# A GpSimd memset behind every gather of a graph kernel's conv passes

## What is computed

```python
eh  = relu(edge_attr @ en1_w.T + en1_b)              # once: [edges, 128]
w_e = (eh @ en2_w.T + en2_b).reshape(-1, 32, 32)     # a 32x32 matrix for every edge
out = h = relu(x @ lin0_w.T + lin0_b)
for _ in range(6):                                   # six conv steps
    msg = einsum('ei,eio->eo', out[src], w_e)        # out[src]: the gather
    agg = segment_sum(msg, dst, num_segments=6250) + conv_bias
    h = out = gru_cell(relu(agg), h)
```

## Time and profile before

| what | value |
|---|---|
| median of the runs | 24,022.46 us |
| profiled execution, first to last instruction (span) | 30,532.6 us |
| GpSimd busy in it | 14,020.9 us (46%), 16,639 instructions |
| of these the gathers, L785 | 9,408, 8,876.9 us |
| TensorE busy | 18,622.1 us (61%) |
| VectorE busy | 11,720.7 us (38%) |
| ScalarE busy | 7,911.3 us (26%) |
| HBM traffic | 110 GB/s over the span |

### The profile page before, as it was taken

One profiled execution on the slowest core, in us unless ns is written; L12 is line 12 of the kernel. 1 busy time (PEld: TensorE's weight loads), 2 busy tenths in 40 slices (PEclk: granted clock), 3 DMA queues, 4 the chain that ended last, 5 costly groups with the idle time before them and its releaser, 6 DMA issues. The chain is left out here.

```text
span 30532.6 us, 420576 instructions
## 1 busy us (share of the span) xinstructions
PE 18622.1 (61%) x121575; PEld 13266.8 (43%) x121575; DVE 11720.7 (38%) x29589; ACT 7911.3 (26%) x20853; POOL 14020.9 (46%) x16639
## 2 busy tenths in 40 slices
PE   3333555555655676667666766676666766676654
PEld 3333322222244454455444554455445544554444
DVE  5444566666710333233323333233323332333220
ACT  0000344445510222222222322232222222232210
POOL 4886355555610444534453445344443445344520
PEclk5555788888977777777777877787777777787777
DMA  3222233322278222112211221122112221122147
GB/s 97 48 49 69 85 122 118 113 99 93 68 293 344 66 64 59 52 58 65 58 54 53 68 63 55 48 69 63 56 53 60 63 59 54 57 65 60 55 142 308
DMA packets 1398480, 2692.30 MB, mean 88 GB/s; under 512 B 938471, under 2 KB 1104704, under 8 KB 1189106
## 3 DMA queue, kind: packets, MB, share of 16 engines
q10 hardware_dynamic: 335568, 1445.71, 13.4%
q1 hardware_dynamic: 709952, 1053.68, 10.0%
q0 software_dynamic: 352256, 186.21, 4.3%
HBM read 2105.10 MB, written 1242.55 MB: 110 GB/s over the span
## 5 line engine op out<-in xcount | busy, mean ns | idle before, releaser
L785 POOL DMA_INDIRECT sb_xg<-node_rows,sb_src_c x9408 | 8876.9, 944 | 11917.8 <-SPq L803 6579.1
L921 PE MATMUL banks<-sb_work,sb_eh_sb 128*128 128x256 f32 x29184 | 8833.9, 453 | 1693.7 <-issue 1358.2
L921 PEld LDWEIGHTS banks<-sb_work,sb_eh_sb 128*128 128x128 f32 x29184 | 6472.3, 229 | 3674.0 <-issue 2259.6
L874 DVE TENSOR_TENSOR sb_work<-sb_xs,banks_p 128x2048 f32<-128x2048 f32 x1824 | 4171.1, 2288 | 9843.7 <-remote 5895.0
L978 ACT ACTIVATE sb_work<-banks 128x512 f32<-128x512 f32 x7296 | 4124.9, 599 | 11185.0 <-remote 7003.8
L1200 PE MATMUL banks<-sb_hot_code,sb_xs 128*128 128x392 bf16 x7296 | 1874.5, 371 | 2173.7 <-DVE sb_work L1163 1435.1
L1163 DVE SCALAR_TENSOR_TENSOR sb_work<-sb_work,sb_eh_sb,banks 128x784 f32 x2432 | 2502.3, 1029 | 572.4 <-PE banks L1202 484.1
L864 DVE COPY sb_xs<-sb_xg 128x32 f32 x14592 | 1762.7, 191 | 2459.9 <-issue 2268.6
L907 PE MATMUL banks_p<-sb_work,sb_en 128*32 128x256 f32 x29184 | 2084.7, 391 | 778.6 <-issue 766.1
L367 POOL DMA_INDIRECT slots<-sb_rows,sb_slot_u x1600 | 2108.6, 1318 | 786.7 <-issue 762.6
L1079 POOL TENSOR_SCALAR sb_xs<-sb_codes,sb_code 128x128 bf16<-128x128 f16 x2432 | 1516.6, 624 | 2067.3 <-PE banks L1202 2067.1
(11 more groups left out here) (281 smaller groups left out, 13084.1 us busy)
## 6 DMA issues: line engine op xcount, KB each, us to landing
sb_eh_sb<-eh ACTq DMA_DIRECT2D x912, 1024.0 KB
weights_between<-sb_work ACTq DMA_DIRECT2D x305, 1568.0 KB
edges_between<-sb_work ACTq DMA_DIRECT2D x305, 1568.0 KB
sb_work<-weights_between SPq DMA_DIRECT2D x147, 3136.0 KB, 12.5
sb_work<-edges_between SPq DMA_DIRECT2D x98, 3136.0 KB, 12.4
eh<-sb_eh_sb ACTq DMA_DIRECT2D x304, 512.0 KB, 2.6
sb_xg<-node_rows,sb_src_c POOLq DMA_INDIRECT x9408
sb_win_row<-window_rows SPq DMA_DIRECT2D x100, 488.3 KB
```

What stands on the lines that cost most here:

```text
L785: nc.gpsimd.indirect_dma_start(m.xg_ring[:, row % RING * D:(row % RING + 1) * D], None, m.node_dram, bass.IndirectOffsetOnAxis(ap=m.src_c[ ...
L874: V.tensor_tensor(m.spread[q], m.xs[h].rearrange("s (t i) -> s t i", i=D)[:, tiles, :].unsqueeze(3) .broadcast_to([P, TS, D, WN]), m.mask_ ...
L921: o = mm(m.ps_pair[u % 4][:, v, :, :], m.eh[h % 2][:, t * K:(t + 1) * K], m.spread[t // TS][:, t % TS, :, :], start=True, stop=True)
```

## The change

Behind each gather GpSimd now writes zeros to one of two scratch tiles of 128x240 f32, in turn, and counts it on a new semaphore `paused`. From the third gather on, it first waits until the memset before last is done. At the end of a pass's gathers it waits for the last memset. Nobody reads the scratch tiles. Nothing else is touched: the gathers, their order, their semaphores and all other engines' programs stay as they are. The scratch tiles take 1,920 bytes of each partition.

```diff
-def gather_rows(nc, m, pool, got, landed, room, held):
+def gather_rows(nc, m, pool, got, landed, room, paused, held):
...
             nc.gpsimd.indirect_dma_start(
                 m.xg_ring[:, row % RING * D:(row % RING + 1) * D], None, m.node_dram,
                 bass.IndirectOffsetOnAxis(ap=m.src_c[:, row:row + 1], axis=0)).then_inc(got[b % L], 16)
+            if row >= 2:
+                pool.wait_ge(paused, row - 1)
+                hold(pool, held)
+            nc.gpsimd.memset(m.pause[row % 2], 0.0).then_inc(paused, 1)
+    pool.wait_ge(paused, JT)
...
-            gather_rows(nc, m, pool, got, landed, room, held_pool)
+            gather_rows(nc, m, pool, got, landed, room, paused, held_pool)
...
         m.own_now = sb("own_now", [P, D], halves=2)
+        m.pause = sb("pause", [P, 240], halves=2)
```

More of the change, by code:

```diff
@@ L810, in conv_pass @@
                "copied", "masked", "twinned", "made", "summed", "g_done", "g_sb", "s_sb", "grouped", "pj_sb", "folded",
-               "out_sb", "held_dve", "held_pool") as (block, *sems):
+               "out_sb", "paused", "held_dve", "held_pool") as (block, *sems):
         got, eh_in, stored = sems[0:4], sems[4:6], sems[6:10]
         (landed, room, copied, masked, twinned, made, summed, g_done, g_sb, s_sb, grouped, pj_sb, folded, out_sb,
-         held_dve, held_pool) = sems[10:26]
+         paused, held_dve, held_pool) = sems[10:27]
         def skewed(eng, *steps, tail=None, behind=0):
```

## The result

The changed kernel takes 25,500.14 us in the median (25,498.74 to 25,516.16) against 24,026.48 us for the kernel before: 1,474 us more. The ratio on record is 1.0617, 95% interval 1.0602 to 1.0632. The forecast was slower, 26,600 us in a range of 24,700 to 27,400: right in its direction and within its range, but the cost of the memsets was put at 2,579 us, 1.75 times what it is.

The account below looks back on a forecast made before the run. GpSimd's gather pace was taken to bound two thirds of every conv loop. Serial memsets raise a loop from 1,998 to 2,428 us, 2,579 us in all on the 24,022.46 us median: 26,600 us, range 24,700 to 27,400.

Parts of the forecast that it names:

- The timed runs have no stalls, and the gathers' pace bounds most of a loop: Conv loops: timed runs lack the profile's burst stalls; gathers bound two thirds of every loop, other engines the first third.
- The calculated loop: One conv loop without stalls: larger of gathers x 1.249 and batches x 11.85 in three stretches, 1,998 us; fill and tail 11.
- The wait and the hold cost nothing: GpSimd's sequencer, per gather: cost zero, as it needs 0.46 of each 1.249 us and the hold takes 17 ns.
- never dry: GpSimd's cores: with the lead cut to two gathers they still have 1.25 us of work; the sequencer needs 0.46.
- The memset's own time, 0.298 us: Per gather on GpSimd: 0.10 us for one column plus 239 x 0.83 ns; between 0.10 and 0.374 us.
- The memset goes serially with the gathers: GpSimd's cores make both, so the gather period becomes 1.249 + 0.298 = 1.547 us; chance 0.70.
- the rival of the gap: The memset fits into the 0.30 us between gathers and costs nothing: 24,022 to about 24,100 us; chance 0.10.
- the forecast's own sum: One loop's three stretches at 1.547 us a gather: 767 + 784 + 876 = 2,428 against 1,998 us; 2,579 us in all.
- The signs that I had listed: Changed kernel's profile: gathers 1.5 to 1.6 us apart if serial, 1.25 to 1.30 with a memset between if that is wrong.
- The stalls rival: Timed runs do stall behind long bursts and the change removes that: loop 1,874 us, time 23,280 us; chance 0.11.
- The port rival: Memsets hold up VectorE's 16 row copies a batch: batch 16.6 us, loop 2,627 us, time 27,800 us; chance 0.05.
- may fall while the time rises: Profiled execution: its stalls, 1,096 us a loop, may shrink, so its span may fall while timed runs get slower.

Follow-up runs that it names:

- the bunched kernels: Against the changed kernel, eight memsets and waits together behind each block of eight gathers: 26,447.27 us; the same on four scratch tiles: 26,103.80 us.
- the size series: Against the changed kernel, only the columns each memset writes differ: 1 column 24,055.62 us, 120 columns 24,619.67 us, 480 columns 27,371.82 us.
- the bunched kernel with four tiles: Eight memsets together behind each block of eight gathers, on four scratch tiles so each waits for the fourth before it: 26,103.80 us, ratio 1.0866.

## Why the prediction was right, and where its size was off

**The timed runs have no stalls, and the gathers' pace bounds most of a loop: shown.** The calculated loop, 1,998 + 11 us, is 2,008 us in the kernel profiled again. I had the batches bind the first third at 11.85 us and gave that stretch 38 us of slack; they bind the first 600 us, at 11.5 us, and the slack is 36 us. The gathers bind the last 1,400 of 2,008 us.

**The wait and the hold cost nothing: nearly.** Their instructions cost nothing (24,018.71 us without memsets). But "never dry" was wrong: with the lead cut to two gathers every 96th gather comes late. In the changed kernel that is 16 x 0.14 = 2 us a loop, some 13 of the 1,474 us, and the bunched kernels show what it can grow to.

**The memset's own time, 0.298 us: 0.312 to 0.316 measured.** Memset of one column plus the iota's slope was a good guide.

**"The memset goes serially with the gathers": this step failed.** I had argued that the whole 0.30 us gap is the gather's own unrecorded part, since the sequencer was up to six gathers ahead and a free core would have begun. The gap is in two parts. For about 0.14 us behind a gather's recorded end the next gather did not start but a memset did; 0.16 us before the next gather's recorded start stay in every kernel. So the rival of the gap was half right, and it was given as all or nothing: a memset of one column fitted, one of some 24 columns would by the estimate above, and one of 240 sticks out by 0.180 us. With 1.4285 us in place of 1.547 the forecast's own sum gives 709 + 724 + 809 = 2,242 us a loop, 244 over 1,998, and 1,464 us in all, against 1,474 measured: the mis-sized term, 0.298 us a gather where 0.180 were measured, is the whole of the miss. The signs that I had listed did not cover 1.43 us: they named 1.25 to 1.30 and 1.5 to 1.6. What GpSimd does in the two parts of the gap is not shown.

**The stalls rival (faster): refuted.** The gathers of the kernel before are 1.249 us apart in an execution that took 24,027.7 us, so no recorded gather was stretched. I should not have taken a feature of one execution for one of the kernel; the arithmetic saved the forecast, not the explanation, which named bursts as the cause.

**The port rival: an effect is there, the price is not.** VectorE's copies of gathered rows, in the kernel before profiled again, in the changed one and with 480 columns (min/median/max in ns):

```profile
L864 DVE COPY sb_xs<-sb_xg x14592: 165/182/440, 9982.3 to 22838.8; 128x32 f32 x200
```

```profile
L869 DVE COPY sb_xs<-sb_xg x14592: 165/215/572, 9976.5 to 24309.6; 128x32 f32 x200
```

```profile
L869 DVE COPY sb_xs<-sb_xg x14592: 160/270/754, 9981.1 to 26181.0; 128x32 f32 x200
```

The median rose from 182 to 215 ns, 0.5 us for the 16 copies of a batch, while a batch waits for its rows anyway. It grows with the memset: 181, 196, 215 and 270 ns with 1, 120, 240 and 480 columns. This is in line with the rule of the Trainium skill ("SBUF — State Buffer", section "Who interferes with whom") that a VectorE copy in its two-port mode and a GpSimd instruction shut each other out; that these copies ran in that mode is not shown. It does not set the time: the size series accounts for it with GpSimd's distance alone.

**The profiled span "may fall while the time rises": it did**, from 30,532.6 to 25,496.6 us, but not by the change's doing.

## What to carry to other kernels

When a profiled span is far over the timed median, rebuild the median from rows that the disturbance can't touch (here a count of gathers times their distance back to back) before reading any wait in it, and profile the kernel again before explaining the disturbance. On an engine that sets the pace, an added instruction costs what sticks out of the gaps that are there, so ask for each gap how much of it the new instruction can use; both "all" and "none" were wrong here. And the same work costs by place: 0.04 us per memset where another chain had slack, 0.18 where the engine bound the loop, 0.26 when bunched, with the late gathers in it. A wait that cuts a sequencer's lead should be tested with the lead really cut; adding its instructions alone does not do that.

## What the runs showed of the hardware that was not expected

- The gap of 0.30 us between two indirect gathers on GpSimd takes in a memset of 0.12 us with no change of the 1.249 us from gather to gather, and about 0.14 us of a longer one; the remaining 0.16 us before a gather stand behind memsets of 120, 240 and 480 columns alike.
- GpSimd's memsets cost 0.12 us for one column and 0.83 ns for each further one of f32; eight of 240 columns in a row take 1.99 us, since they start 0.24 us apart though each is recorded with 0.31 us.
- Where a wait held GpSimd's sequencer to a lead of two gathers, every 96th gather came 0.47 us late with 1 column, 0.34 with 120, 0.14 with 240 and not with 480. In the bunched kernel with four tiles it was 1.33 us late. In the kernel before, and with memsets left out, it was as a rule on time. The cause is open.
- A program's profiled execution can be 27% longer than its timed ones and the next profiled execution of the same program not at all (30,532.6 and 24,025.9 us). All other profiled executions of this study were within 20 us of their kernels' medians. The cause is open.
